# Half 1's second layer norm turned by VectorE blocks and an HBM scratch instead of 16 TensorE transposes

## The reference, cut to what matters

```python
x = x + xattn(layernorm(x), ids, ctx, ctx, ctx)     # 4 experts, picked by token id
n = layernorm(x)                                    # the second norm
scores = sigmoid(n @ router_w.T)
idx = top_k(scores + e_bias, 4)
w = scores[idx] / (scores[idx].sum() + 1e-20)
routed = sum_e w[:, e] * (silu(n @ gate_e.T) * (n @ up_e.T)) @ down_e.T      # 16 experts, 96 wide
shared = silu(n @ sg.T) * (n @ su.T) @ sd.T                                  # 96 wide
x = x + routed + shared
```

## Time and profile before

| | us |
|---|---|
| median of three runs (173.77 to 174.3) | 173.8 |
| the profiled execution, its own time | 173.89 |
| its span in the trace | 171.8 |
| TensorE busy | 166.6 (97% of the span) |
| DVE / ACT / POOL busy | 114.2 / 67.8 / 39.6 |

### The profile page before, as it was taken

One profiled execution on the slowest core, in us unless ns is written; L12 is line 12 of the kernel. 1 busy time (PEld: TensorE's weight loads), 2 busy tenths in 40 slices (PEclk: granted clock), 3 DMA queues, 4 the chain that ended last, 5 costly groups with the idle time before them and its releaser, 6 DMA issues.

```text
span 171.8 us, 2194 instructions
## 1 busy us (share of the span) xinstructions
PE 166.6 (97%) x728; PEld 130.6 (76%) x728; DVE 114.2 (66%) x230; ACT 67.8 (39%) x112; POOL 39.6 (23%) x37
## 2 busy tenths in 40 slices
PE   6989999999999999999999999999999999999992
PEld 2568888888877888788787778788787887878881
DVE  0779778888984988588688528964744444444452
ACT  2472520551258254824664593152212222223320
POOL 2593000698200025539385000000000000000000
PEclk9999999999999999999999999999999999999999
DMA  4999000176400036742111200043361211100003
GB/s 137 307 373 352 23 4 2 25 236 227 122 0 4 15 130 181 203 160 67 61 61 61 61 0 4 8 126 126 113 195 45 75 65 61 62 0 4 2 0 122
DMA packets 7971, 16.41 MB, mean 95 GB/s; under 512 B 1336, under 2 KB 2200, under 8 KB 7832
## 3 DMA queue, kind: packets, MB, share of 16 engines
q1 hardware_dynamic: 7960, 16.27, 29.0%
HBM read 15.08 MB, written 1.18 MB: 95 GB/s over the span
## 4 chain that ended last, share of the span: by engine, by line
PE 97%; ACT 0%; POOL 0%; DVE 0%; issue 0%; DVEq 0%; POOLq 0%
PE bank L853 26%; PE bank L913 14%; PE bank L911 13%; PE bank L912 13%; PE bank L931 7%; PE bank L934 7%; PE bank L932 7%; PE bank L943 4%; PE bank L820 2%; PE bank L907 1%; PE bank L908 1%; PE bank L832 1%; ACT xn_hi L433 0%; POOL warm L383 0%; DVE xt L732 0%
## 5 line engine op out<-in xcount | busy, mean ns | idle before, releaser
L913 PE MATMUL bank<-xn_lo,gu_hi 128*128 128x512 f32 (+1 forms) x104 | 41.0, 394 | 0.0
L911 PE MATMUL bank<-xn_hi,gu_lo 128*128 128x512 f32 x96 | 37.9, 395 | 0.0
L912 PE MATMUL bank<-xn_hi,gu_hi 128*128 128x512 f32 x96 | 37.8, 394 | 0.0
L501 ACT ACTIVATE h_hi<-hid 128x512 fp32r<-128x512 f32 (+1 forms) x26 | 16.4, 632 | 45.7 <-DVE hid L720 45.7
L725 DVE TENSOR_TENSOR h_lo<-hid,h_hi 128x512 fp32r<-128x512 f32 (+1 forms) x26 | 20.2, 778 | 15.6 <-ACT h_hi L501 15.6
L913 PEld LDWEIGHTS bank<-xn_lo,gu_hi 128*128 128x128 f32 (+1 forms) x104 | 19.4, 186 | 5.0
L491 ACT ACTIVATE act_sb<-bank 128x512 f32<-128x512 f32 (+1 forms) x26 | 15.4, 594 | 18.1 <-PE bank L913 18.0
L398 POOL TENSOR_TENSOR gu_lo<-stage,gu_hi 128x512 fp32r<-128x512 f32 x12 | 17.9, 1516 | 17.6 <-ACT gu_hi L426 17.6
L912 PEld LDWEIGHTS bank<-xn_hi,gu_hi 128*128 128x128 f32 x96 | 18.0, 187 | 4.4
L911 PEld LDWEIGHTS bank<-xn_hi,gu_lo 128*128 128x128 f32 x96 | 18.0, 187 | 4.4
L931 PE MATMUL bank<-h_hi,wd_lo 128*128 128x512 f32 (+1 forms) x52 | 20.6, 396 | 0.0
(11 more groups left out here) (76 smaller groups left out, 213.1 us busy)
## 6 DMA issues: line engine op xcount, KB each, us to landing
stage<-gu_d SPq DMA_DIRECT2D x6, 512.0 KB, 3.5
stage<-wd_d SPq DMA_DIRECT2D x3, 512.0 KB, 4.1
x<-comb_d SPq DMA_DIRECT2D x8, 192.0 KB, 2.7
ids<-comb_d SPq DMA_DIRECT2D x8, 192.0 KB, 3.0
stage<-ctx_d SPq DMA_DIRECT2D x4, 256.0 KB, 5.0
xt<-xt_d SPq DMA_DIRECT2D x1, 1024.0 KB, 10.3
x<-comb_d SPq DMA_DIRECT2D x8, 128.0 KB, 3.1
ids<-comb_d SPq DMA_DIRECT2D x8, 128.0 KB, 2.8
```

The costliest lines, as they stand in the source:

```text
L911: nc.tensor.matmul(out[:], gu_lo[:, cols], xn_hi[:, h, k], start=(k == 0), stop=False)
L912: nc.tensor.matmul(out[:], gu_hi[:, cols], xn_hi[:, h, k], start=False, stop=False)
L913: ins = nc.tensor.matmul(out[0:rows, :], gu_hi[:, wide], xn_lo[:, h, k], start=False, stop=(k == KC - 1))
```

## The change

Both TensorE turns of half 1's second norm go. In their place:

- at the end of g = 1 DVE turns `xt`'s half 1 in 32x32 blocks into the upper half of `x` (`turn_x1`, 2 instructions); SP writes it to the HBM scratch `x1_d` (4 DMAs) and reads it back token-major (4 DMAs), which puts the blocks where they belong;
- the statistics move from g = 3 to g = 5, the application from g = 5 to g = 6;
- ahead of g = 7's product DVE turns `xn` in 32x32 blocks (`turn_xn`, 4 instructions), and SP writes it to `xn_d` (4 DMAs) and reads it back feature-major into `xn` (2 DMAs); ACT's `x_high` and DVE's `x_low` read it there, and no longer in PSUM;
- ACT's two copies (`copy_x1`) go;
- item (1, 0) moves from g = 9 to g = 11 (`early = 10`); the first item of half 1 that needs its routing weights stays at g = 14;
- `normalise_scores(1, mark_best(1))` moves from behind `hidden_2` of the second position after (1, 0) to ahead of `product` of the first one after it;
- GpSimd raises half 1's variances to the power -1/2 after low parts 9 to 12, before it was after 9 and 10.

```diff
+X1_TURN, X1_WRITE, X1_READ, X1_STATS, X1_APPLY = 1, 5, 7, 5, 6
+XN_TURN, XN_WRITE, XN_READ = 7, 11, 12
...
-        early = 8
+        early = 10
...
+            def write_x1():
+                sp.wait_ge(x1_turned, KC)
+                rows = x1_d.rearrange("(b j) (q c) -> q j b c", j=LANES, q=QUARTERS)
+                blocks = x[:, TT:].rearrange("p t d -> p (t d)").rearrange("p (b c) -> p b c", c=KC * LANES)
+                for q in range(QUARTERS):
+                    sp.dma_start(rows[q], blocks[q * LANES:(q + 1) * LANES]).then_inc(x1_out, 16)
+
+            def read_x1():
+                sp.wait_ge(x1_out, QUARTERS * 16)
+                rows = x1_d.rearrange("(b t j) f -> b j t f", t=TT, j=LANES)
+                for b in range(QUARTERS):
+                    sp.dma_start(x[b * LANES:(b + 1) * LANES, TT:], rows[b]).then_inc(x1_back, 16)
+
+            def write_xn():
+                sp.wait_ge(xn_turned, TT)
+                rows = xn_d.rearrange("q k i (b c) -> b i (q k) c", c=P)
+                blocks = x[:, TT:].rearrange("p t d -> p (t d)").rearrange("p (m c) -> p m c", c=P)
+                for b in range(QUARTERS):
+                    sp.dma_start(rows[b], blocks[b * LANES:(b + 1) * LANES]).then_inc(xn_out, 16)
+
+            def read_xn():
+                sp.wait_ge(xn_out, QUARTERS * 16)
+                for k in range(KC):
+                    sp.dma_start(xn_turn[:, k], xn_d[:, k]).then_inc(xn_back, 16)
...
-            low_part(early_pieces)
-            low_part(early_pieces + 1)
+            for n in range(early_pieces, early_pieces + 4):
+                low_part(n)
             rstd_of(3, 5)
...
-                act.wait_ge(side_done, side_at[what, h, k] + 1)
+                wait_features(act, what, h, k)
...
-                if g == X1_AT + 1:
-                    copy_x1(1)
...
+            def turn_x1():
+
+                dve.wait_ge(x1_done, HALVES * KC)
+                dve.wait_ge(normed_a, HALVES * TT // 2)
+                for k in range(KC):
+                    nc.vector.transpose(x1_blocks[:, k], xt[:, k, HALF:].rearrange("p (b j) -> p b j", j=LANES)).then_inc(x1_turned, 1)
+
+            def turn_xn():
+
+                dve.wait_ge(normed_a, NORMS * TT // 2)
+                dve.wait_ge(normed_v, NORMS * TT // 2)
+                for t in range(TT):
+                    nc.vector.transpose(xn_blocks[:, t], xn[:, t].rearrange("p (m i) -> p m i", i=LANES)).then_inc(xn_turned, 1)
...
+                if g == XN_TURN:
+                    turn_xn()
+                if g == place[1, 0] + 1:
+                    normalise_scores(1, mark_best(1))
                 product(g)
                 hidden_2(g)
                 if g == place[1, 0]:
                     turn_logits(1)
-                if g == place[1, 0] + 2:
-                    normalise_scores(1, mark_best(1))
...
-                if g == place[1, 0] - 2:
-                    norm_transposes("n2", 3, 1)
-
                 if g >= LAG and downs_at[g - LAG]:
                     for n in downs_at[g - LAG]:
                         down(n)
-                if g == X1_AT:
-                    x1_transposes(1, 0)
-                    x1_transposes(1, 1)
```

More of the change, by code:

```diff
@@ L58 @@
 LANES = 32
-X1_AT = 2
+QUARTERS = P // LANES
+X1_TURN, X1_WRITE, X1_READ, X1_STATS, X1_APPLY = 1, 5, 7, 5, 6
+XN_TURN, XN_WRITE, XN_READ = 7, 11, 12
 SPREADS = 4
@@ L130, in build @@
         comb_row = sb("comb_row", [P, HALVES, P])
+        x1_blocks = x[:, TT:].rearrange("p t d -> p (t d)").rearrange("p (b k i) -> p k b i", k=KC, i=LANES)
+        xn_blocks = x[:, TT:].rearrange("p t d -> p (t d)").rearrange("p (m t i) -> p t m i", t=TT, i=LANES)
+        xn_turn = xn[:].rearrange("p t d -> p (t d)").rearrange("p (k c) -> p k c", k=KC)
+        x1_d = nc.dram_tensor("x1_d", (HALF, D), F32, kind="Internal").ap()
+        xn_d = nc.dram_tensor("xn_d", (QUARTERS, KC, LANES, HALF), F32, kind="Internal").ap()
         comb_d = nc.dram_tensor("comb_d", (HALVES, LANES, HALF), F32, kind="Internal").ap()
@@ L147, in build @@
         rows_out, rows_turned = [sem(f"rows_out{h}") for h in range(HALVES)], sem("rows_turned")
-        comb_zero, x1_copied = sem("comb_zero"), sem("x1_copied")
+        comb_zero = sem("comb_zero")
+        x1_turned, x1_out, x1_back = sem("x1_turned"), sem("x1_out"), sem("x1_back")
+        xn_turned, xn_out, xn_back = sem("xn_turned"), sem("xn_out"), sem("xn_back")
         dstep = sem("dstep")
@@ L214, in side_bank, with features, wait_features @@
             return bank[side_order[side_at[what, h, c]][3]]
+        def features(what, h, k):
+            return xn_turn[:, k] if (what, h) == ("n2", 1) else side_bank(what, h, k)[:]
+        def wait_features(eng, what, h, k):
+            if (what, h) == ("n2", 1):
+                eng.wait_ge(xn_back, KC * 16)
+            else:
+                eng.wait_ge(side_done, side_at[what, h, k] + 1)
         def widths(c):
@@ L375, in _ @@
                     load_piece(len(pieces) - 2 + (g == 6))
+                if g == X1_WRITE:
+                    write_x1()
+                if g == X1_READ:
+                    read_x1()
+                if g == XN_WRITE:
+                    write_xn()
+                if g == XN_READ:
+                    read_xn()
                 if g == place[1, SPREADS]:
@@ L414, in _ @@
             rstd_of(2, 4)
-            low_part(early_pieces)
-            low_part(early_pieces + 1)
+            for n in range(early_pieces, early_pieces + 4):
+                low_part(n)
             rstd_of(3, 5)
-            for n in range(early_pieces + 2, len(pieces)):
+            for n in range(early_pieces + 4, len(pieces)):
                 low_part(n)
@@ L428, in x_high @@
             def x_high(what, h, k):
-                act.wait_ge(side_done, side_at[what, h, k] + 1)
+                wait_features(act, what, h, k)
                 if what == "n2":
                     act.wait_ge(z_done, (mixed[1, h, KC - 1] + 1) * E1)
-                nc.scalar.activation(xn_hi[:, h, k], side_bank(what, h, k)[:], ACT.Copy).then_inc(xhi_done, 1)
+                nc.scalar.activation(xn_hi[:, h, k], features(what, h, k), ACT.Copy).then_inc(xhi_done, 1)
             def first_z(n):
@@ L463, in score @@
                 nc.scalar.preload_act_table(ACT.Silu)
[L465 to L472, removed]
             def router_logits(h):
@@ L553, in _ @@
                 hid_high(g)
-                if g == 5:
+                if g == X1_APPLY:
                     apply_norm(3)
@@ L600, in x_low @@
                 dve.wait_ge(xhi_done, n + 1)
-                dve.wait_ge(side_done, side_at[what, h, k] + 1)
-                nc.vector.tensor_tensor(xn_lo[:, h, k], side_bank(what, h, k)[:], xn_hi[:, h, k].bitcast(F32),
+                wait_features(dve, what, h, k)
+                nc.vector.tensor_tensor(xn_lo[:, h, k], features(what, h, k), xn_hi[:, h, k].bitcast(F32),
                                         ALU.subtract).then_inc(xlo_done, 1)
@@ L796, in _ @@
                 hid_low(g)
-                if g == 3:
+                if g == X1_TURN:
+                    turn_x1()
+                if g == X1_STATS:
                     for t in range(TT):
```

11 lines of the change are left out of this document (2 added, 9 removed).

## The result

The changed kernel is slower by 1.4%, clear of the noise: 176.32 us (176.21 to 176.82) against 173.83 (173.77 to 174.3) on the same chip, a ratio of 1.0143 [1.0117, 1.0169]. Forecast was 172.6 and a range up to 174.4. The profiled execution took 176.40, 2.51 more than the one of before.

What follows compares the result with a forecast made beforehand. TensorE was taken as the bound. 1.75 us of transposes removed and 0.6 us given back at item (1, 0), the rest hidden, make -1.15 us: 173.8 to 172.6 us, with a range of 171.9 to 174.4.

Steps and rivals of the forecast that it cites:

- What bounds the kernel: Whole span: TensorE, busy 97%, never stands after warm-up; a removed matmul saves its step, an added wait costs its length.
- What is removed: TensorE: 16 transposes of half 1 go, 1.75 us, all on the path; ACT's two copies are worth 0.
- The x1 round trip: DVE turn, scratch write and read of x1: back by 79.1, statistics want it at 80.5, so cost 0.
- The rival of the small packets: x1's scratch write: packets above 42 ns delay xn's landing; 174.9 at 60 ns, 178.7 at 90 ns; 13%.
- The xn turn: DVE's turn_xn behind the application: ends at 89.0 us (87.6 to 91.2), with one hit by GpSimd counted.
- The xn round trip: xn's scratch: write 4.0 us, two reads on four DMA engines 7.7 us, so xn is back at 100.7.
- What this costs TensorE: Gate of item (1, 0): can start at 101.5 instead of 100.85, so 0.6 us (0 to 4) given back.
- The second rival, gain given back: xn's path: another GpSimd hit, slower packets and a later landing make the wait 2.2; 173.3 to 174.3 us; 17%.
- The marks and the power, cost 0: Half 1's marks have 0.4 us slack before up of g = 14; GpSimd's power ends before g = 6's round: both 0.
- All of the gain: Rival: xn's reads run on 16 engines or DVE is 0.6 us earlier, no wait appears, 172.05 us; 25%.

Runs made afterwards that it cites:

- experiment 1: Changed kernel with the scratch xn_d laid out anew so that each of xn's two reads has 128 rows outermost: 172.09 us.
- experiment 2: Changed kernel with each of xn's two reads split into four DMAs of 32 rows, scratch layout left alone: 171.93 us.
- experiment 4: Changed kernel keeping only x1's round trip; xn turned by 8 TensorE transposes as before, output not the reference's: 173.33 us.
- experiment 10: Experiment 1's kernel with GpSimd's power put back ahead of low parts 11 and 12: 177.45 us.
- experiment 7: Changed kernel with low parts 13 and 14 one position later, so GpSimd's work is off the application: 173.89 us.
- experiment 5: Changed kernel with half 1's statistics, application, turn_xn and xn's write and read one position earlier: 177.28 us.
- experiment 6: Experiment 5's kernel with SP's write and read of xn one place earlier still: 174.51 us.
- experiment 3: Changed kernel with 11 bf16 matmuls of no use added on TensorE ahead of the gate of item (1, 0): 175.25 us.
- experiment 9: Experiment 1's kernel with half 1's marks back behind hidden_2 of the second position after item (1, 0): 177.66 us.

## Why the prediction was wrong, point by point

- **What bounds the kernel** held in that TensorE is the bound. "A wait put in costs its full length" did not: it costs more where the clock falls, and that is the flaw below.
- **What is removed, 1.75 us** held to 0.01: experiments 1 and 2 have lengths 1.76 and 1.74 below before.
- **The x1 round trip, cost 0** held (experiment 4), and DVE's 512-column transposes took 0.686 us each, 0.7 forecast. The statistics started at 81.06 without a wait. But the cover was thinner than the 1.4 us or more of the working. The working had 2 us for a read's landing; it was up to 5.4 (experiment 4). The last of the four was issued at 74.9, so x1 was back by 80.3 and not by 79.1; in experiment 10 the statistics waited 0.2 us for it. The rival of the small packets (13%) fell.
- **The xn turn, 89.0** was 90.1. Half of that was there when the statistics started (81.06, not 80.5), half was a second GpSimd hit; one had been counted and two were in the stretch, within the 0 to 2.2 us given. Experiment 7 shows that GpSimd's place decides it. The Trainium skill ("SBUF — State Buffer", "SBUF: two separate sides") says that the shared port pair is held for a whole instruction; here that holds for an operation of 128x4, 0.15 us alone and 1.24 beside GpSimd.
- **The xn round trip**: reading four engines out of the count of small packets was right, and it was the decisive reading. The Trainium skill ("DMA: Bandwidth & Descriptors", "Rules for kernel authors") says that an outermost dimension below 16 confines a DMA to at most as many engines; 25.1% agrees, and experiments 1 and 2 mend it. Packets took 90 ns (25.1% of 16 x 4 us over 178 of them), 95 forecast; but what lies around them was 2.9 us and not 1.6, which had been taken from a small write. In experiments 5 to 7 the read took 8.8 to 9.8 us.
- **What this costs TensorE: "Given back: 0.6 us"** is the step that failed, in two ways. Its size: the landing came 1.80 us later (turn +1.13, write -0.27, read +0.94), and the ideal start was 100.60 and not 100.85, as this execution reached g = 1 earlier, which makes the wait 2.7. The gate started 0.8 us behind the landing, as forecast, but its first products then lost 0.27 more to the low parts. Both together lie inside the 0 to 4 given; but the date was built from the middle of three uncertain terms, each of which goes straight to TensorE; and the final range, up to 174.4, has room for only 2.35 us given back, not for 4. And it lacked a term: behind the gap the clock was at half for 3.4 us, 1.54 us more. By the working's own sum, 173.8 - 1.75 + 2.70 + 0.27 is 175.0, and the clock's term makes it 176.6; measured are 176.3. Experiment 3 shows that this term comes from the gap, and that a kernel with the same landing is rid of it when TensorE is kept at work. The Trainium skill ("TensorE: Matmul & The Clock Gate", "Why this matters for your kernels") warns that idle gaps between matmuls bring the clock down, but means longer ones than this; in the trace 2.70 us were enough for 1.00 to fall to 0.50.
- **The second rival, gain given back**, had the right place and a wait that was not far off (2.2, at worst 3.8), and gave 173.3 to 174.3 for it. It too stopped short of the clock; with the clock's 1.54 it would have read 174.8 to 175.8.
- **The marks and the power, cost 0** held for the change, whose traces show no wait at either place. Experiments 9 and 10 price what is gone without the new places, against experiment 1: 5.6 and 5.4 us in medians, and 7.3 and 6.3 us of length in the profiled executions, which took longer than their medians.
- **All of the gain, 172.05 (25%)** is what experiment 1 measured, 172.09, by the mechanism that this rival named.

What stays open: why the four-engine read took 9.7 and 9.8 us in experiments 5 and 6 and 8.6 in the changed kernel (the broadcasts beside it are a likely reason; no run had the read without them), and why half clock lasted 3.4 us in one place and 6.8 in another. It is not the kernel alone: the mean clocks of experiment 10's executions fall into two groups, and in experiment 9 the profiled one had 0.981 and the other three 0.989 to 0.990, which is what the changed kernel has with 3.4 us.

## What to carry to other kernels

Where TensorE never stands, a wait put in front of it is to be priced as its length plus what the clock takes behind it: here 2.7 + 1.5 us. A step may end close to the date at which TensorE wants it, closer than the spread of the terms of its date. Then it is no saving until there is slack. For any DMA, look which dimension stands outermost on both sides, since the DMA share, and in a quiet stretch the count of small packets, show how many engines work: one relabelling of a scratch tensor turned 1.4% slower into 1.0% faster, and 171.93 and 172.09 us are the best versions seen. And what a moved step pushes later (statistics) moves whatever waits for it in another queue (GpSimd's power, SP's broadcasts): these have to move along.

## What the runs showed of the hardware

- Gaps of TensorE of 1.3 and 1.5 us left the granted clock at 1.00. Gaps of 2.7 and 3.3 us went with half clock for 3.4 us, one of 3.4 us and a pair of 1.7 and 2.4 with 1.5 us of work between them with 6.8 us in the profiled executions. The clock fell 0.8 us after TensorE had started again in the changed kernel, and within the gap in experiments 5, 9 and 10. No row of waits has it.
- 512 KB in 2 KB packets took 8.6 us over four engines (98 GB/s, flat) and at most 3.7 us over sixteen. A 192 KB broadcast issued behind the read landed after 7.4 us in the first case and 3.2 in the second.
- x1's four scratch writes to HBM, 512 packets of 256 bytes each, landed 2.8 to 2.9 us after their issue; the reads of the same bytes took 4.7 to 5.4, with weights and broadcasts beside them.
- DVE's 32x32 block transposes of fp32: 312 ns for 128 columns, 402 to 405 (medians) for 256, 686 for 512.
- DVE's operation on 128x4 took 0.15 us alone and 1.24 to 1.25 beside GpSimd's low parts, and its 128x512 low part 0.69 and 1.25 to 1.26 (experiment 7 against the changed kernel and experiments 1 to 3).
